# Graph kernel on one core: layer 0 by a dense matrix that one pass builds together with the one of layers 2 and 3

## The reference, cut to what matters

```python
# layer 0: three steps
norm = dis[src] * edge_weight * dis[dst]
out = clip(0.9 * segment_sum(norm[:, None] * out[src], dst) + 0.1 * x, 0, 1)   # 3 times
# layer 1: six steps of an edge network and a GRU
eh = relu(edge_attr @ en1_w.T + en1_b)                  # 128 numbers for each edge
msg = einsum('ei,eio->eo', out[src], (eh @ en2_w.T + en2_b).reshape(-1, 32, 32))
h = gru(relu(segment_sum(msg, dst) + conv_bias), h)      # 6 times
# layers 2 and 3: one degree-normed sum over the edges each
agg = segment_sum(x[src], dst)
```

## Time and profile before

| | us |
|---|---|
| median of 3 runs | 32663.71 |
| lowest, highest | 32643.08, 32664.95 |
| the profiled execution: time | 32413.36 |
| the profiled execution: span | 32411.6 |
| TensorE busy | 18026.4 (56% of the span) |
| GpSimd busy | 15499.2 (48%) |
| VectorE busy | 11934.9 (37%) |
| ScalarE busy | 6546.6 (20%) |

### The profile page before, as it was taken

One profiled execution on the slowest core, in us unless ns is written; L12 is line 12 of the kernel. 1 busy time (PEld: TensorE's weight loads), 2 busy tenths in 40 slices (PEclk: granted clock), 3 DMA queues, 4 the chain that ended last, 5 costly groups with the idle time before them and its releaser, 6 DMA issues. The chain is left out here.

```text
span 32411.6 us, 403512 instructions
## 1 busy us (share of the span) xinstructions
PE 18026.4 (56%) x104961; PEld 13157.7 (41%) x104961; DVE 11934.9 (37%) x35567; ACT 6546.6 (20%) x20858; POOL 15499.2 (48%) x15719
## 2 busy tenths in 40 slices
PE   3334332333344447665766576667666766676654
PEld 3333221221211125544554455445544554455444
DVE  5443222222477754332333233323332333233320
ACT  0000111111111113222322232223222322232210
POOL 5884466456444544453445344534453445344520
PEclk5555555655555558777877787778777877787777
DMA  3223121111122112221221122212221222122137
GB/s 95 49 49 86 47 56 46 52 54 50 45 80 69 49 32 70 63 56 48 70 63 56 49 70 62 56 49 69 62 57 49 69 62 56 51 69 62 56 114 317
DMA packets 1256771, 2157.89 MB, mean 67 GB/s; under 512 B 744415, under 2 KB 1032120, under 8 KB 1116522
## 3 DMA queue, kind: packets, MB, share of 16 engines
q10 hardware_dynamic: 423840, 1341.95, 12.1%
q0 software_dynamic: 502784, 263.58, 5.7%
q1 hardware_dynamic: 329576, 546.81, 4.9%
HBM read 1721.40 MB, written 761.91 MB: 77 GB/s over the span
## 5 line engine op out<-in xcount | busy, mean ns | idle before, releaser
L772 POOL DMA_INDIRECT sb_xg<-node_rows,sb_src_c x14112 | 13388.5, 949 | 14651.7 <-SPq L790 8683.5
L908 PE MATMUL banks<-sb_work,sb_eh_sb 128*128 128x256 f32 x29184 | 8441.9, 446 | 1103.5 <-issue 818.4
L861 DVE TENSOR_TENSOR sb_work<-sb_xs,banks_p 128x2048 f32<-128x2048 f32 x1824 | 4170.8, 2288 | 9736.7 <-remote 7067.5
L908 PEld LDWEIGHTS banks<-sb_work,sb_eh_sb 128*128 128x128 f32 x29184 | 6400.2, 226 | 2796.2 <-issue 1360.2
L965 ACT ACTIVATE sb_work<-banks 128x512 f32<-128x512 f32 x7296 | 4133.6, 599 | 11173.8 <-remote 7697.2
L894 PE MATMUL banks_p<-sb_work,sb_en 128*32 128x256 f32 x29184 | 2207.2, 394 | 1024.0 <-issue 1008.2
L851 DVE COPY sb_xs<-sb_xg 128x32 f32 x14592 | 1769.5, 193 | 2391.2 <-issue 2228.5
L365 POOL DMA_INDIRECT slots<-sb_rows,sb_slot_u x1600 | 2108.2, 1318 | 785.3 <-issue 756.9
L935 PE MATMUL banks_s<-sb_fold,sb_pj 128*128 128x32 f32 x1824 | 421.6, 305 | 3391.1 <-ACT sb_pj L977 2913.2
L1370 PE MATMUL banks<-sb_hot_code,sb_hot_row 128*128 128x392 bf16 x2432 | 1170.5, 506 | 1816.8 <-DVE sb_hot_code L1318 1330.6
L1155 PE MATMUL banks_s<-sb_fold,sb_s 128*128 128x32 f32 x608 | 192.0, 409 | 3251.3 <-DVE sb_s L1094 2989.6
(11 more groups left out here) (284 smaller groups left out, 14777.9 us busy)
## 6 DMA issues: line engine op xcount, KB each, us to landing
sb_eh_sb<-eh ACTq DMA_DIRECT2D x912, 1024.0 KB
adjacency<-sb_work ACTq DMA_DIRECT2D x153, 3136.0 KB
sb_work<-adjacency SPq DMA_DIRECT2D x98, 3136.0 KB, 12.3
sb_xg<-node_rows,sb_src_c POOLq DMA_INDIRECT x14112
eh<-sb_eh_sb ACTq DMA_DIRECT2D x304, 512.0 KB
sb_win_row<-window_rows SPq DMA_DIRECT2D x100, 488.3 KB
slots<-sb_zeros SPq DMA_DIRECT2D x19, 2368.0 KB
sb_rowin<-slots SPq DMA_DIRECT2D x152, 296.0 KB, 3.2
```

Source lines behind the costliest of these rows:

```text
L772: nc.gpsimd.indirect_dma_start(m.xg_ring[:, row % RING * D:(row % RING + 1) * D], None, m.node_dram, bass.IndirectOffsetOnAxis(ap=m.src_c[ ...
L861: V.tensor_tensor(m.spread[q], m.xs[h].rearrange("s (t i) -> s t i", i=D)[:, tiles, :].unsqueeze(3) .broadcast_to([P, TS, D, WN]), m.mask_ ...
L908: o = mm(m.ps_pair[u % 4][:, v, :, :], m.eh[h % 2][:, t * K:(t + 1) * K], m.spread[t // TS][:, t % TS, :, :], start=True, stop=True)
```

## The change

The building of the matrix moves out of step 2 to the front of layer 0, and the same pass builds a second matrix, the edge weights between the nodes. All three steps of layer 0 are then `dense_pass` over that second matrix. `plain_pass` and `adjacency_pass` go, and with them the gathers of layer 0 and its three `add_tiles`. The encoding of the edges, which was spread over two passes, comes into the one pass, `build_cells`.

An edge weight is written as the sum of three bf16 numbers (`name_cells` splits it). For each tile

- GpSimd writes two one-hot blocks of 128x128 in bf16, one of edges that count in the second matrix and one of all;
- ScalarE writes three blocks of 128x128, the second of GpSimd's times each part of the weight;
- VectorE writes one block, 128x392;
- PE does four matmuls of 392 columns: three, added up, for the weights and one for the counts, into two neighbouring PSUM banks;
- VectorE adds both products in one instruction of 784 columns.

There are two such pairs of PSUM banks instead of four banks, eight of each 128x128 block and four of VectorE's. A slot is now 8 windows, 98 slots of both matrices; a flush writes 2 x 1.6 MB. The encoder's operations stand once in each half batch: transposes before its 8 tiles on PE, encoder matmuls behind them; the bias on VectorE after the fifth add of the next half; ReLU, the store of `eh` and the flush on ScalarE behind the weighted blocks of the next half. SP fetches the attributes straight from their places, 128 bytes at a time.

```diff
 BLOCKS = NQ * NM // P
-CODES, CELLS = BLOCKS * WN, BLOCKS * P
+HALF = P // 2
+CODES, CELLS = BLOCKS * WN, BLOCKS * HALF
 SLOTS, THIRDS, HOTS = NW // LO, 3, 4
+KEPT = THIRDS * 2 * CELLS + HALF
 FULL = NODES // NM
 REST = NODES - FULL * NM
 assert EQ * ET == EDGES and TP >= EDGES // P + NW and JT * P >= EDGES and JT % 4 == 0 and OQ * OC == TP and NW == NQ * NC and 2 * EC == TC and NB * PW == NM
...
             step(V.tensor_tensor(m.cell[:, :], m.cell[:, :], meta[:, :, 0], ALU.add))
-            step(V.tensor_tensor(m.cell[:, :], m.cell[:, :], meta[:, :, 2], ALU.mult))
+            step(V.tensor_scalar(m.cell_j[:, :], m.cell_i[:, :], P - 1, None, ALU.bitwise_and))
+            step(V.tensor_copy(m.src_t[:, :], m.cell_j[:, :]))
+            step(V.scalar_tensor_tensor(m.src_t[:, :], meta[:, :, 2], -float(P), m.src_t[:, :], ALU.mult, ALU.add))
             step(V.tensor_scalar_add(code[:, :, 4], m.cell[:, :], -1.0))
-            step(V.tensor_scalar(m.cell_j[:, :], m.cell_i[:, :], P - 1, None, ALU.bitwise_and))
...
+            halves = m.cell_j.bitcast(BF16)
...
+            step(V.tensor_copy(high, meta[:, :, 1]))
+            step(V.tensor_tensor(m.cell[:, :], meta[:, :, 1], high, ALU.subtract))
+            step(V.tensor_copy(middle, m.cell[:, :]))
+            step(V.tensor_tensor(m.low[:, :], m.cell[:, :], middle, ALU.subtract))
+            step(V.tensor_copy(weight[:, :, 2], high))
+            step(V.tensor_copy(weight[:, :, 3], middle))
             step(V.tensor_copy(m.codes[:, :], m.iota[:, 0:CODES]))
...
-def plain_pass(nc, m, weight, after, encode=None):
...
-def adjacency_pass(nc, m):
+def build_cells(nc, m):
...
+        @block.sync
+        def _(sp):
+            for i, n, h in batches(sp):
+                for q in range(2):
+                    if not first(i, h):
+                        sp.wait_ge(turned, 2 * n + q - 1)
+                        hold(sp, held_sp)
+                    sp.dma_start(m.attr[q].rearrange("s (t f) -> s t f", f=D),
+                                 slots_v[:, bass.ds(n * TC + q * EC, EC), META:ROW]).then_inc(rows_in[q], 16)
...
+            for i, n, h in batches(pool):
...
+                G.tensor_copy(pair(own_code), halves(F16)[:, :, 4:6]).then_inc(ready, 1)
+                G.tensor_copy(pair(own_weight), halves(BF16)[:, :, 2:4]).then_inc(ready, 1)
+                G.tensor_copy(own_low, m.low[:, bass.ds(n * TC, TC)]).then_inc(ready, 1)
...
+                for t in range(TC):
+                    if t % HOTS == 0 and not (first(i, h) and t < 2 * HOTS):
+                        pool.wait_ge(tabled, n * TC + t - HOTS)
+                        hold(pool, held_pool)
+                    G.tensor_scalar(m.hot_row[0][:, t % (2 * HOTS), :], m.codes[:, 0:P], own_code[:, 2 * t + 1:2 * t + 2], None,
+                                    ALU.is_equal)
+                    G.tensor_scalar(m.hot_all[t % (2 * HOTS)], m.codes[:, 0:P], m.row_now[h % 2][:, t:t + 1], None,
+                                    ALU.is_equal).then_inc(rows_hot, 1)
...
+            def flush(i, b, g):
...
+                act.wait_ge(added, b * TS)
+                for k in range(2):
+                    act.dma_start(m.cells_dram[k][bass.ds(row, P), :], m.cells[:, bass.ds(third + k * CELLS, CELLS)],
+                                  cond=done).then_inc(flushed[g % 2], 16)
...
+            def rectify(c):
+                act.wait_ge(biased, c + 1)
+                nc.scalar.activation(m.eh_now, m.eh_now, ACT.Relu).then_inc(relu, 1)
+                act.wait_ge(relu, c + 1)
+                act.dma_start(m.eh_dram[:, bass.ds(c * EC * K, EC * K)], m.eh_now).then_inc(eh_out, 16)
...
+                    c = n * 2 + q
+                    act.wait_ge(turned, c + 1)
+                    if not first(i, h):
+                        act.wait_ge(encoded, c - 1)
+                    nc.scalar.activation(m.attr_t[q], m.ps_turn[q], ACT.Copy).then_inc(turned_sb, 1)
+                    for t in range(q * TS, q * TS + TS):
+                        act.wait_ge(rows_hot, n * TC + t + 1)
+                        if not (first(i, h) and t < 2 * HOTS):
+                            act.wait_ge(tabled, n * TC + t - 2 * HOTS + 1)
+                        for k, w in enumerate((m.weight[h % 2][:, 2 * t:2 * t + 1], m.weight[h % 2][:, 2 * t + 1:2 * t + 2],
+                                               m.low_now[h % 2][:, t:t + 1])):
+                            r = nc.scalar.activation(m.hot_row[1 + k][:, t % (2 * HOTS), :], m.hot_all[t % (2 * HOTS)],
+                                                     ACT.Copy, scale=w)
+                        r.then_inc(weighted, 1)
+                    if not (first(i, h) and q == 0):
+                        rectify(c - 1)
+                        flush(i, c, 2 * h + q)
+            rectify(2 * BATCHES - 1)
...
+                return m.cells[:, bass.ds(place, 2 * CELLS)].rearrange("p (s x) -> p s x", x=HALF)[:, :, 0:WN]
...
+            def bias(c, early):
+                dve.wait_ge(encoded, c + 1)
+                if not early:
+                    dve.wait_ge(eh_out, c * 16)
+                V.tensor_tensor(m.eh_now.rearrange("s (g x) -> s g x", g=2), m.ps_encoded,
+                                m.en1_b[:, :].unsqueeze(1).broadcast_to([P, 2, 4 * K]), ALU.add).then_inc(biased, 1)
...
                 def name(t):
-                    if t >= HOTS:
+                    if not (first(i, h) and t < HOTS):
                         dve.wait_ge(tabled, n * TC + t - HOTS + 1)
-                    V.tensor_scalar(m.hot_row[t % HOTS], m.codes[:, 0:P], m.code[h % 2][:, 2 * t + 1:2 * t + 2], None,
-                                    ALU.is_equal).then_inc(hot, 1)
                     V.tensor_scalar(m.hot_code[t % HOTS], m.codes[:, :], m.code[h % 2][:, 2 * t:2 * t + 1], None,
-                                    ALU.is_equal).then_inc(hot, 1)
+                                    ALU.is_equal).then_inc(codes_hot, 1)
                 def add(t):
...
+                    V.scalar_tensor_tensor(here, here, m.keep[:, bass.ds(n * TC + t, 1)], m.ps_both[t % 2],
                                            ALU.mult, ALU.add).then_inc(added, 1)
...
+                    q = t // TS
+                    if t % TS == 0 and not first(i, h):
+                        dve.wait_ge(flushed[1 - q], 32 * n)
...
                         name(t + ahead)
                     add(t)
-            skewed(dve, (masks, 0), (add_cells, 0))
+                    if t % TS == TS // 2 and not (first(i, h) and q == 0):
+                        bias(n * 2 + q - 1, first(i, h) and q == 1)
+            bias(2 * BATCHES - 1, False)
...
+            for i, n, h in batches(pe):
+                for q in range(2):
+                    c = n * 2 + q
+                    pe.wait_ge(rows_in[q], n * 16 + 16)
+                    if not first(i, h):
+                        pe.wait_ge(turned_sb, c - 1)
+                    for g in range(2):
+                        mt = nc.tensor.transpose(m.ps_turn[q][:, g * P:(g + 1) * P], m.attr[q][:, g * P:(g + 1) * P],
+                                                 m.ident[:, :])
+                    mt.then_inc(turned, 1)
+                    for t in range(q * TS, q * TS + TS):
+                        pe.wait_ge(weighted, n * TC + t + 1)
+                        pe.wait_ge(codes_hot, n * TC + t + 1)
+                        if not (first(i, h) and t < 2):
+                            pe.wait_ge(added, n * TC + t - 1)
+                        code = m.hot_code[t % HOTS]
+                        for k in range(3):
+                            mm(m.ps_cells[t % 2][0], m.hot_row[1 + k][:, t % (2 * HOTS), :], code,
+                               start=(k == 0), stop=(k == 2))
+                        mm(m.ps_cells[t % 2][1], m.hot_row[0][:, t % (2 * HOTS), :], code, start=True,
+                           stop=True).then_inc(tabled, 1)
+                    pe.wait_ge(turned_sb, c + 1)
+                    if not (first(i, h) and q == 0):
+                        pe.wait_ge(biased, c)
+                    for g in range(2):
+                        me = mm(m.ps_encoded[:, g, :], m.attr_t[q][:, g * P:(g + 1) * P], m.en1[:, :], start=True, stop=True)
+                    me.then_inc(encoded, 1)
...
+def dense_pass(nc, m, matrix, own_dram, after):
...
+                sp.dma_start(m.slot_cells[h], m.cells_dram[matrix][bass.ds(n * 2 * P, 2 * P), :]
+                             .rearrange("(g p) c -> p g c", p=P)).then_inc(slot_in[h], 16)
...
+                    last = mm(m.ps_dense[h][D * j:D * (j + 1), :], m.x_rows[:, b * D:(b + 1) * D],
+                              m.slot_cells[h][:, :, b * HALF:(b + 1) * HALF], start=(b < 4),
+                              stop=((own_dram is None or j != 1) and b >= BLOCKS - 4))
+                if own_dram is not None:
+                    pe.wait_ge(named, n + 1)
```

(59 more changed lines are left out.)

357 lines of the change are left out of this document (77 added, 280 removed).

## The result

The changed kernel takes 30546.9 us (median of 4 runs, 30526.7 to 30574.6), the kernel before 32664.3 (4 runs, 32643.1 to 32691.1): a ratio of 0.9351, 95% interval 0.9338 to 0.9363. The forecast was 30880 us in a range of 29700 to 32100. 2117 us were saved where I had said 1784. One execution is left out of the numbers of this text, because it took over 1.5% more than the others of its kernel: 34999 us, in the run with two matmuls a tile.

The account below looks back on a forecast made before the run. No engine was full in layer 0's old steps; GpSimd's gathers, then VectorE, were busiest. Profiled 32413 - 8579 + 1344 + 37, with 5426 for the loop, is 30641, at ratio 1.0077 30880 us; range 29700 to 32100.

Parts of the forecast that it names:

- Removed, and the dense passes: Layer 0: old plain passes, third step and adding of parts go, 8579 us; three dense passes of 448 us come, 1344 us.
- The loop: New pass building both matrices in layer 0: 35.7 us for each of 152 batches, 5426 us.
- the clock decides most; I take the middle: Building loop: PE's clock rises and falls again, so the mean of 34.4 us a batch (1.2 GHz) and 26.9 (2.4 GHz).
- clock stays up: Rival for the building loop: PE keeps its higher clock, 32.0 us a batch, 30310 us in all; chance 0.22.
- The flush: Seam between half batches: VectorE waits for the matrix write, 3.2 (6.4 at 2.4 GHz) us in 98 of 304 halves.
- 9 to 11 us, under 13.45: ScalarE's work per half batch, 9 to 11 us, claimed hidden under the 13.45 us a half takes at 2.4 GHz.
- Tile and seam: Building loop: VectorE 1.26 us per tile; serial seam between halves, 3.9 us of PE plus 1.4 of ScalarE at 1.2 GHz.
- 0.4 us a comparison: GpSimd in the building loop: 32 comparisons and 2 us make 15 us a batch, hidden; spacing 0.3 to 0.5 us expected.
- the rival with its price on: GpSimd bounds the building loop at 0.95 us a comparison: about 40.5 us a batch, 31610 us; chance 0.23 with the port.
- the slower case: Building loop: at 1.42 us a GpSimd comparison a batch takes 47.4 us and everything saved is gone; chance 0.07.
- the port: Building loop: each VectorE code block waits for a GpSimd operation, 6.4 us on top of 35.7; chance 0.23 with GpSimd.
- The scale: Whole kernel: profiled execution to median of timed runs, times 1.0077, taking 30641 to 30880 us.

## Why the prediction was right, and where its terms were off

**Removed, and the dense passes.** 8579 us out and 1345 in, as forecast.

**The loop, 5147 us against 5426.** Two errors of opposite sign, so that the total came nearer than its terms: that part is luck. Forecast for a batch were (34.4 + 26.9) / 2 + 2 = 32.7 us besides the flush and 3.1 for its stall. Measured are 28.1 (4269 / 152) with the flush early; what its late place costs beyond that is 4.1 of stall (626 / 152), 1.2 of ScalarE's queue (189 / 152) and 0.3 in the tiles. The first error, 4.6 too much, is my "the clock decides most; I take the middle". The granted clock did fall in the run with two matmuls (0.58), but I expected it to fall again by itself. In the changed kernel it mostly fell behind a stall: of 1.34 ms at the lower level in the loop, 1.02 ms lie between the last add before one of the 97 flush seams and the end of the half behind it, and with the flush moved the loop's mean is 0.98. The batch with the flush early is that of the rival "clock stays up" (26.9 and 1 of idle time). The whole, 33.8, lies between that rival's 32.0 and my 35.7.

**The flush.** The stall was right as a mechanism and, at the clock that the loop had, as a size: 6.4 us in 98 halves were forecast for the higher level, 6.45 in 97 are measured, where my mean of both levels had 3.1 us a batch for 4.1. That it lands some 8 us after its issue was right too (6003.3 to 6012.1 is 8.8). What I missed is ScalarE's queue ahead of the copy: the register load, some 2.1 us from one DMA issue to the next in each of 304 halves and also when nothing is flushed, with the copy for the next half behind it. I had counted it only as ScalarE's busy time, "9 to 11 us, under 13.45", hence hidden. It costs 1.2 us a batch that stood at nothing in my sum. An engine whose busy time is short can be late if its short work stands in a row behind one late wait, here the bias after the fifth add.

**Tile and seam.** Adds 1.26 us apart, 1.03 us long: as worked out. The 1.4 us that ScalarE adds to the seam are seen with the flush early (1.35 to 1.50 us) and at the usual seam of the changed kernel (median 1.5); where a flush is issued or a body begins it is 2.2 to 5.3.

**GpSimd.** Taken 0.4 us a comparison, measured 0.58 between starts, inside the bounds of 0.22 and 0.95 though not in the 0.3 to 0.5 that I had named as a sign, and hidden as said. A price half again as high changed nothing because GpSimd had 2067 us to spare. The run with twice the comparisons is the rival with its price on: at 2 x 0.58 = 1.16 us per block a batch took 39.4 us where 32 x 1.16 + 2 gives 39. So the formula behind the break-even at 1.42 us, which I named for the slower case, holds up to 1.16; and the 40.5 us that I gave the rival at 0.95 us were too many, since flush and idle time hide behind GpSimd when it is the bound. (For the port the working gave 35.7 + 6.4 = 42.1, not 40.5.) A cost of GpSimd's work for VectorE is there, 19 ns on a code block (339 against 320): 46 us in all if nothing hid it. SBUF — State Buffer, Who interferes with whom (the Trainium skill), says that a VectorE operation in a two-port mode and a GpSimd operation lock each other out. In the mean of these runs that would be a twentieth of a code block, and the rival's 6.4 us a batch were 0.3. GPSIMD Engine Reference (the Trainium skill), 3.1, gives 1.8 to 2.6 cycles an element, an estimate of 1.5 to 2.2 ns at the 1.2 GHz of its example. The measured 2.5 ns a column are a little more, and the fixed 0.29 us come on top.

**The scale.** The step from the profiled execution to the median, times 1.0077, added 239 us, because the timed runs of before were that much above its profiled one. It came to nearly the right amount for a reason that I had not looked at. Layer 1 and the rest, the same code, took 20412 us in before's profile and 20596 in after's; in the four later runs on that kind of chip its first and last norms are 20509 to 20636 us apart, in before's profile 20363 and in after's 20547. So before's profile was a short sample of a part that varies by over 1%, and 184 of the 239 us are that part at its usual length; scaling the new loop and the dense passes with it had no ground, since the changed kernel's profiled execution (30534) and median (30547) agree within 13 us. Of the 333 us by which the forecast was too high, 279 are the loop, 12 small terms and 42 the scale (239 - 184 - 13).

## What to carry to other kernels

Cost an engine by its queue, not by its busy time: write down what stands behind its latest wait, register loads and skipped DMAs included, and who waits for the last item; moving one conditional store some four tiles forward was worth 868 us, more than the whole rewrite on that kind of chip (661). Ask of a clock forecast what will interrupt the engine, since a stall costs itself and then a little of the pace behind it (626 and 46 us here), and less work for the engine need not gain any. Read a seam off all its copies and not off one: the one seam with 5.3 us of pause was that of a loop body's end. And a saving that consists of removed work is worth what that work costs on the chip at hand: the new loop took the same time on both kinds within 0.2% (5125, 5130 and 5135 us), the old plain passes differed by a quarter.

## What was not expected of the hardware

Chips of two kinds ran one and the same program in 32.7 and 24.7 ms, with nearly equal instruction durations; the difference is in the parts that gather, where on the slower kind TensorE at times pauses 1.2 to 1.9 us between matmuls with no wait that the profile shows and GpSimd waits longer for room. Taking away half of TensorE's tile matmuls gained nothing (granted clock 0.58, encoder matmuls 1010 ns for 648). A register load before a conditional transfer held ScalarE's queue for some 2.1 us, also where nothing was transferred, and the branch at the end of a loop body for 2.4 to 3.2 us (about 6 behind a flush just issued). A comparison of 16 columns on GpSimd takes 0.33 us, one of 128 columns 0.60.
